# Two groups of the last batch's K projected four pairs of heads later, and the first feed-forward weights loaded one pair later

## The reference

```python
x = x + tanh(g_xattn[0]) * xattn0(layernorm(x), ctx, ctx, mask)   # q, k, v projections, softmax(q k / sqrt(32) + mask) v
x = x + tanh(g_ffn[0]) * ffn0(layernorm(x))                       # 512 -> 2048 gated, two 2048 x 2048 layers, -> 512
x = x + tanh(g_xattn[1]) * xattn1(layernorm(x), ctx, ctx)         # as xattn0 without mask, then Wo
x = x + tanh(g_ffn[1]) * ffn1(layernorm(x))                       # quantized gate, up and down
```

## Time and profile before

| | us |
|---|---|
| median of 3 runs | 1626.61 (1623.2 to 1630.42) |
| profiled execution | 1621.03 |
| its span, first to last instruction | 1619.2 |
| granted clock, mean | 0.994 |
| PE busy in the span | 1571.7 (97%) |
| DVE, ACT, POOL busy | 1027.8, 970.6, 392.3 |

### The profile page before, as it was taken

How to read it: one execution, slowest core, us unless ns; L and a number is a source line. 1 busy time by engine, 2 the same in 40 slices (tenths; PEclk the granted TensorE clock), 3 DMA queues, 4 the chain that set the end, 5 groups by cost and what they waited for, 6 DMA issues and landing times.

```text
span 1619.2 us, 25557 instructions
## 1 busy us (share of the span) xinstructions
PE 1571.7 (97%) x9262; PEld 1430.9 (88%) x9262; DVE 1027.8 (63%) x1828; ACT 970.6 (60%) x2006; POOL 392.3 (24%) x540
## 2 busy tenths in 40 slices
PE   6999999999988999999999999999999999999898
PEld 5899899899977999999999997889989999997654
DVE  5477777787786553223644425737777777778786
ACT  4477667677765455444544434457667767777565
POOL 3111211212133222222222222311111111213740
PEclk9999999999999999999999999999999999999999
DMA  8575767676572225554365643576576667666400
GB/s 233 138 192 153 200 165 193 162 196 174 142 200 81 92 92 180 173 189 164 105 227 195 218 147 111 167 179 178 153 187 172 170 153 200 158 161 170 156 13 30
DMA packets 146164, 257.77 MB, mean 159 GB/s; under 512 B 40833, under 2 KB 90113, under 8 KB 145900
## 3 DMA queue, kind: packets, MB, share of 16 engines
q1 hardware_dynamic: 145580, 255.82, 55.9%
q10 hardware_dynamic: 448, 0.14, 0.0%
HBM read 187.49 MB, written 58.57 MB: 152 GB/s over the span
## 4 chain that ended last, share of the span: by engine, by line
PE 91%; DVE 3%; ACT 2%; issue 1%; POOL 1%; DMA 1%; SPq 1%; DVEq 0%; ACTq 0%; POOLq 0%
PE ps L1012 32%; PE ps L718 17%; PE ps L714 15%; PE ps L780 8%; PE ps L768 8%; PE ps L841 2%; PE ps L754 2%; PE ps L757 2%; PE ps L953 2%; PE ps L966 1%; PE ps L878 1%; PE ps L756 1%; PE ps L755 1%; DMA QT<-in_wv 1%; ACT P L1617 1%
## 5 line engine op out<-in xcount | busy, mean ns | idle before, releaser
L1012 PE MATMUL ps<-ah_f,wh_f 128*128 128x400 f32 (+1 forms) x1296 | 443.4, 343 | 0.9 <-issue 0.8
L1012 PE MATMUL ps<-al_f,wh_f 128*128 128x400 f32 (+1 forms) x1296 | 442.2, 342 | 0.0
L1935 POOL TENSOR_TENSOR cxl<-raw,cxh 128x384 fp32r<-128x384 f32 (+1 forms) x112 | 105.6, 964 | 616.5 <-ACT cxh L1575 616.5
L1508 DVE TENSOR_TENSOR wl_f<-raw_f,wh_f 128x1024 fp32r<-128x1024 f32 x85 | 103.9, 1224 | 235.9 <-POOL wh_f L2155 235.9
L1012 PEld LDWEIGHTS ps<-ah_f,wh_f 128*128 128x128 f32 x1296 | 243.5, 188 | 2.4 <-issue 1.5
L1012 PEld LDWEIGHTS ps<-al_f,wh_f 128*128 128x128 f32 x1296 | 243.8, 188 | 0.0
L1142 DVE TENSOR_REDUCE nmax<-ps 100x1 f32<-100x722 f32 x256 | 220.8, 904 | 32.5 <-PE ps L756 29.0
L1617 ACT ACTIVATE P<-ps,nmax 100x722 f32<-100x722 f32 x256 | 220.2, 862 | 31.8 <-DVE nmax L1142 31.7
L1629 ACT ACTIVATE PT<-ps 128x400 fp32r<-128x400 f32 x384 | 166.2, 505 | 77.1 <-PE ps L768 76.0
L1868 ACT ACTIVATE raw_f<-wl_f 128x1024 f32<-128x1024 f32 x88 | 93.5, 1062 | 175.5 <-DVE wl_f L1508 175.5
L1148 DVE TENSOR_TENSOR PT<-ps,PT 128x400 fp32r<-128x400 f32 x384 | 196.5, 568 | 3.2
(11 more groups left out here) (194 smaller groups left out, 2503.0 us busy)
## 6 DMA issues: line engine op xcount, KB each, us to landing
KS<-kd SPq DMA_DIRECT2D x192, 361.0 KB
raw_f<-in_h SPq DMA_DIRECT2D x64, 512.0 KB, 4.5
raw_f<-in_gud SPq DMA_DIRECT2D x48, 512.0 KB, 4.4
raw<-in_ctx SPq DMA_DIRECT2D x64, 192.0 KB, 3.7
raw_f<-in_w SPq DMA_DIRECT2D x24, 512.0 KB, 3.7
kd<-ksh SPq DMA_DIRECT2D x60, 192.0 KB, 2.1
kd<-ksl SPq DMA_DIRECT2D x60, 192.0 KB, 2.4
raw<-in_ctx SPq DMA_DIRECT2D x64, 169.0 KB, 4.2
```

The costliest lines, as they stand in the source:

```text
L1012: return e.matmul(o, p, q, start=start, stop=stop)
L1508: e.tensor_tensor(wl[:, z, :], raw[:, r, :], raw32(wh[:, z, :]), ALU.subtract).then_inc(v_ul, 1)
L1935: e.tensor_tensor(m.cx[1][:, k, off:off + n], m.raw[:, k, off:off + n], raw32(m.cx[0][:, k, off:off + n]), ALU.subtract).then_inc(g_cx, 1)
```

## The change

Attention 0 gets its own list of jobs for pairs 52 to 58. Four half groups of K of batch 7 move: group 2 half 0 from 52 to 56, group 2 half 1 from 55 to 57, group 3 half 0 from 53 to 57, group 3 half 1 from 56 to 58. `load_k` of groups 2 and 3 of batch 7 moves from SP's iterations 56 and 58 to 58 and 59, the four `fetch` from 57 to 58. GpSimd prepares units in 59, 60, 61 and splits in 58 to 61 and 62. Attention 1 keeps its order; the index tables become one per layer. No operation is added or removed.

```diff
+LAST_BESIDE = {52: (("k", 1, 0, 1),), 53: (("k", 1, 1, 1),), 55: (("v", 1, 4),), 56: (("v", 0, 5), ("k", 0, 2, 0)),
+               57: (("k", 0, 2, 1), ("k", 0, 3, 0)), 58: (("k", 0, 3, 1),)}
...
-def beside(i):
+def beside(i, L):
 
     if i >= NP:
         return []
-    return [(j[0], i // 8 + j[1]) + j[2:] for j in BESIDE[i % 8] if i // 8 + j[1] < B]
+    jobs = LAST_BESIDE.get(i, BESIDE[i % 8]) if L == 0 else BESIDE[i % 8]
+    return [(j[0], i // 8 + j[1]) + j[2:] for j in jobs if i // 8 + j[1] < B]
...
-                    if p in (0, 2):
-                        load_k(L, m, b, 2 + p // 2)
+                    if p in ((2, 3) if L == 0 and b == B - 1 else (0, 2)):
+                        load_k(L, m, b, 2 if p == (2 if L == 0 and b == B - 1 else 0) else 3)
...
-                    if L == 0 and i == 57:
+                    if L == 0 and i == 58:
                         w.wait_ge(p_job, NJOB)
                         w.wait_ge(p_pv, 56)
                         w.wait_ge(g_cx, 56)
...
-                    if L == 0 and i in (58, 60, 61):
-                        prepare((i - 57) // 2)
+                    if L == 0 and 59 <= i < 62:
+                        prepare(i - 59)
                     if L == 0 and out_at(i) is not None:
                         batch_root(out_at(i))
-                    if L == 0 and 57 <= i < 61:
-                        split_kept(i - 57)
+                    if L == 0 and 58 <= i < 62:
+                        split_kept(i - 58)
```

More of the change, by code:

```diff
@@ L126, in group_of @@
     return [n < n1 for _, n1 in groups].index(True)
-JOBS, RINGS = list(FIRST), [list(FIRST), list(FIRST)]
+JOBS, RINGS = [list(FIRST), list(FIRST)], [list(FIRST), list(FIRST)]
 for _i in range(NP + 1):
-    JOBS += beside(_i)
     for _l in range(2):
+        JOBS[_l] += beside(_i, _l)
         if scaled_at(_i) is not None:
@@ L139 @@
             RINGS[_l].append(("xn", turned_at(_i)))
-        RINGS[_l] += beside(_i)
+        RINGS[_l] += beside(_i, _l)
         if _l and _i in OUT_AT:
@@ L148 @@
 RINGS[1].append(("out", TILES - 1))
-NJOB = len(JOBS)
-JOB = {j: i for i, j in enumerate(JOBS)}
+NJOB = len(JOBS[0])
+JOB = [{j: i for i, j in enumerate(jobs)} for jobs in JOBS]
 def half_of(j):
     return j[3] if j[0] == "k" else j[2] // 3
-LAST_OF = {(j[1], half_of(j)): i for i, j in enumerate(JOBS)}
+LAST_OF = [{(j[1], half_of(j)): i for i, j in enumerate(jobs)} for jobs in JOBS]
 PLACES = [{i: r for r, i in enumerate(ring)} for ring in RINGS]
@@ L539, in attention @@
                         spread_q(L, m, b + 1)
-                    for j in beside(i):
+                    for j in beside(i, L):
                         if j[0] == "k":
@@ L610, in store_k @@
                 off, size = HALF[half]
-                w.wait_ge(v_job, NJOB * L + JOB["k", b, g, half] + 1)
+                w.wait_ge(v_job, NJOB * L + JOB[L]["k", b, g, half] + 1)
                 if n >= 4:
@@ L740, in ring_free @@
                     else:
-                        w.wait_ge(v_job, NJOB * L + JOB[old] + 1)
+                        w.wait_ge(v_job, NJOB * L + JOB[L][old] + 1)
                 def scores(i):
@@ L774, in weigh @@
                     w.wait_ge(v_t, 3 * (NP * L + i) + 3)
-                    w.wait_ge(v_job, NJOB * L + JOB["v", b, KT - 1] + 1)
+                    w.wait_ge(v_job, NJOB * L + JOB[L]["v", b, KT - 1] + 1)
                     ring_free(("pv", i))
@@ L1124, in low_job @@
                     o = job_out(m, j, ring_bank(L, j))
-                    w.wait_ge(a_job, NJOB * L + JOB[j] + 1)
+                    w.wait_ge(a_job, NJOB * L + JOB[L][j] + 1)
                     if j[0] == "k":
@@ L1573, in high_ctx @@
                         if b:
-                            w.wait_ge(p_job, NJOB * L + LAST_OF[b - 1, half] + 1)
+                            w.wait_ge(p_job, NJOB * L + LAST_OF[L][b - 1, half] + 1)
                         e.activation(m.cx[0][:, k, off:off + n], m.raw[:, k, off:off + n], ACT.Copy).then_inc(a_cx, 1)
@@ L1578, in high_job @@
                     o = job_out(m, j, ring_bank(L, j))
-                    w.wait_ge(p_job, NJOB * L + JOB[j] + 1)
+                    w.wait_ge(p_job, NJOB * L + JOB[L][j] + 1)
                     if j[0] == "k":
@@ L1751, in attention @@
                         weights(2 * i + 2)
-                    if len(beside(i)) < 2 and i + 1 < NP:
+                    if len(beside(i, L)) < 2 and i + 1 < NP:
                         weights(2 * i + 3)
@@ L1755, in attention @@
                         high_normal(KEPT)
-                    for j in beside(i)[:1]:
+                    for j in beside(i, L)[:1]:
                         high_job(j)
-                    if len(beside(i)) == 2 and i + 1 < NP:
+                    if len(beside(i, L)) == 2 and i + 1 < NP:
                         weights(2 * i + 3)
@@ L1765, in attention @@
                         high_ctx(b + 2, 0, range(2 * p - 12, 2 * p - 10))
-                    for j in beside(i)[1:]:
+                    for j in beside(i, L)[1:]:
                         high_job(j)
```

## The result

| | before | after |
|---|---|---|
| median of 20 runs | 1626.15 us (1619.7 to 1630.42) | 1630.47 us (1625.04 to 1636.97) |
| profiled execution | 1621.03 | 1628.49 |
| its span | 1619.2 | 1626.7 |
| granted clock, mean | 0.994 | 0.989 |

The changed kernel is slower: ratio 1.0029, 95% interval 1.0017 to 1.0042, or 4.3 us (2.8 to 6.8). The sign was forecast and the time lies in the range; the forecast size, +2 us, lies under the interval.

The account below looks back on a forecast made before the run. PE bounds the kernel, except a three-engine loop in the last iterations. Parts 1 to 3 +1.9, part 4 0, part 5 +0.3: +2.2, taken +2, so 1628.6 us; range 1621.5 to 1635.

Parts of the forecast that it names:

- What bounds it: Attention 0's last pairs: PE bounds iterations 52 to 56; 57 and 58 idle 2.23 and 1.37 us in a three-engine loop.
- Part 1: Iterations 52 to 58: moving 7.96 us of PE jobs fills idle time, bringing scores 60 3.5 us earlier if nothing else moved.
- the charge of 0.5: Iterations 52 and 53: 0.5 us charged for nearing the 4.4 us engine loop with ACT's and DVE's job work behind it.
- Part 2: Scores 60: the third group's late K load lands at t + 15.2, wanted t + 12.0; a 3.2 us stall, bounds 2.0 to 4.5.
- t: Start of iteration 57, at scores 58; forecast about 462.0 instead of 467.34.
- Part 3: Scores 62: the fourth group's load, queued behind the weights, lands at 490.0; a second stall of 3.3 us (2.4 to 3.9).
- the 1.0 taken back in iteration 61: Iteration 61, 5.60 us before: 1.0 us recovered because ACT finishes its bias and measurement during the stall.
- Part 4: FFN 0's preparation: later weights through GpSimd cost 0, under about 2 us of cover; without the cover up to 3.
- Part 5: PE's clock in the last pairs: low stretch again, a little longer; from -0.5 to +3 us, taken +0.3.
- rival C: Iterations 59 to 62: stalls drop the clock before about 480, PE bounds them; +6.6, 1633.2 us, or 1638; chance 0.15.
- Rival A: K loads come in time or cost under 1 us each, idle time is filled; -3, 1623.6 us; chance 0.22.
- Rival B: DVE and ACT hold iterations 52 to 55 at about 5.3 to 6, both stalls stay; +4, 1630.6 us; chance 0.13.

Follow-up runs that it names:

- the experiment with both loads freed: Changed kernel, but third and fourth groups' loads take the second group's copy, issued earlier, the fourth's ahead of the weights; ratio to before 0.9998, median 1625.26 us.
- the pair of kernels with the small load: Changed kernel, fourth group's load bringing 64 of 722 columns, without and with 20 extra PE matmuls before scores 60; ratios 1.0032 and 1.0025.

## Why the prediction was right, point by point

**What bounds it.** Right: PE's idle time was what could be won, and the experiment with both loads freed won 3.6 us of it at scores 62, as the 2.23 and 1.37 of the earlier trace rows promised.

**Part 1.** Iteration 52, iterations 53 and 54 together, 55 and 56 took 5.24, 11.35, 5.66 and 7.69 us, 0.87 more in sum than the terms without the charge of 0.5. The charge was about the size, in part by luck: at the end of iteration 54 scores 56 waited for a load of K too (0.32, and 0.55 in the second profile). The shorter iterations brought these scores forward by 4.5 us, their load by only 1.6 (issued at 441.25 instead of 442.86). The prediction didn't look at the loads of the first group. Scores 60 were due 11.98 us into iteration 57, as said (12.0).

**Part 2.** Right in mechanism and place; the load was issued at t + 8.8 (8.6 forecast). The failing term is the length of the load: 7.9 us from issue to scores, not 6.6. The stall was 4.67 and 4.74 us, not 3.2, and a little over the upper bound of 4.5, which had the fourth group's store ahead in the queue. That store is only part of the 1.3 us missing in the length: with the load put ahead of it, the load still took 7.4. What the rest is stays open.

**Part 3.** The load of the fourth group landed when forecast: scores 62 started at 490.01 and 490.12 (490.0 forecast). But the stall of 3.3 us was 0 in one profile and 2.85 in the other. In the first the low clock had already delayed PE to the same moment: the load's last data moved between 489.5 and 490.0. The position was right and what fills it was not: I treated stall and clock as two things that add. Where PE reached scores 62 sooner, the load shows itself more fully (waits of 5.91, 4.61, 4.64 and 8.93 us in four kernels). Of the 1.0 taken back in iteration 61 one profile shows 0.2 and the other nothing (5.38 and 5.77 us against 5.60).

The Trainium skill, "DMA: Bandwidth & Descriptors", section "Queues, rings and completion order", says that each DMA engine takes descriptors in ring order. The traces agree: with 1 MB of weights moved behind the load, the wait of 4.64 us at scores 62 was gone in both profiles of that kernel.

**Part 4.** Right for the changed kernel: POOL waited 2.61 us for the statistics before the root, so the cover was there (about 2 forecast), and the last split ended at 504.3 (504.2 forecast). Of the two kernels in which the cover was gone one lost 2.6 us by GpSimd's chain (up to 3 forecast), the other at most 0.24.

**Part 5.** The term that was most mis-sized. I took +0.3; the pair of kernels with the small load puts it at 2.3 us, in the upper part of my range (+3). Against the kernel before, which has a low stretch of its own, iteration 59 to FFN 0's first product took 1.6 us longer in the first profile (28.45 against 26.86), with no wait for a load in it. This was rival C's mechanism, and its turning point, a clock that falls before about 480, was met: it fell at 478.2. In the first profile it took the place of part 3's stall, so the sum moved less than C's 6.6: the tail +3.1 and +3.9 in two profiles, against +1.9 + 0.3 forecast, and +4.3 us in the medians. The forecast's case and C are thus both in the result; the forecast named the late loads, C the length of iterations 59 and 60 (5.81 and 5.89 us, where C's terms give about 5.2 for the first and 6.1 for the second).

**How much was luck.** The sum came near in part because errors offset each other. Up to scores 60 the changed kernel lost 1.5 us in the first profile, where the forecast had it 0.3 ahead. Behind them it lost 1.6, all of it without a wait for the fourth group's load, where the forecast had 2.2 for that load and 0.3 for the clock. Of the signs named, full iterations 57 and 58, scores 60 near 477.5 (478.31) and scores 62 later than 487 came true in both profiles, the wait at scores 62 in one. No low stretch was longer than 12 us.

**Rival A** fell: the loads took 7.9 us, not under 3.4. **Rival B** fell: iterations 52 to 55 became 5.24 us shorter, of the 6.08 us of PE work that left them.

**Left open.** Whether the 4.3 us of the medians hold more than the tail's 3.1 to 3.9 can't be told within the interval. The tail of the kernel before is known from one profile. Where the low clock falls behind scores 62 differs between profiles, and was not controlled. Why stretches of lower clock in the unchanged attention 1 move from profile to profile was not tried.

## What to carry to other kernels

Work that fills an engine's idle time late in a stage is free only if nothing made from it has still to travel. Before moving it, count from its last matmul through the stores, the queue and the load to its reader: here 4.8 us from the half's last matmul to the load's issue and 7.9 for the load, against 8.0 until its scores. Look at all transfers of the queue: behind the one late load stood a second, hidden one, and behind that a third chain through GpSimd, and each took over when the one before was cured. In a queue like this one, where the late load ran behind the weights issued before it, put the small load that someone waits for ahead of the large one that nobody needs yet, and split the large one if need be.

## What the hardware showed that I had not expected

- A stall of 4.67 us came with 10.2 us of half clock, and the two iterations behind it took 11.70 us, against 9.48 in the kernel that kept PE busy in the stall. The length varies: behind the stall of 4.74 us in the second profile of the same kernel it was 6.9 us (476.5 to 483.4).
- A store of half a group, issued at 474.09 behind a load, had landed by 479.25, when SP went on to the load that waits for it: 5.2 us. The same kind of store with no load ahead of it took 2.5 us (460.18 to 462.69). So a full queue is paid for twice, by the store and by the load.
- Fourteen profiles took 1114.8 to 1124.9 us for the same code behind FFN 0's first product. A single profile's total says nothing about 3 us; its tail says more, since two profiles of one kernel differed there by 0.8 us (75.04 and 75.81) and 1.1 us (69.83 and 68.74).
